# Longer TensorE filler and three moved steps around the gate columns of an mLSTM block (two-layer decoder, one core)

## The reference

```python
x = ln(x + causal_attention(x))
x = ln(x + cross_attention(x, ctx, mask))
x = ln(x + sign_mlp(x))                  # 256 -> 1024 -> 1024 -> 256, weights +1 and -1
x = ln(x + performer(x))                 # causal linear attention, 16 heads
x = ln(x + mlstm(x, ctx, ctx))
x = ln(x + quantised_conv_mlp(x))

def mlstm(q, k, v):
    gate_in = concatenate([q, k, v], -1)
    it = gate_in @ Wi_w.T + Wi_b;  ft = gate_in @ Wf_w.T + Wf_b
    csum = cumsum(log_sigmoid(ft), over tokens)
    D = where(causal, csum_i - csum_j + it_j, -inf)
    max_d = max(D, -1);  D = exp(D - max_d)
    C = (q_h @ k_h.T) * D / sqrt(32)
    H = C @ v_h / (max(abs(sum(C, -1)), exp(-max_d)) + 1e-6)
    return group_norm(H per head) * gn_w + gn_b
```

## Time and profile before

| | |
|---|---|
| median of 3 runs | 926.52 us |
| lowest and highest | 925.8 and 930.36 us |
| the profiled execution | 926.52 us, span 925.3 us |
| mean granted clock of TensorE | 0.949 of 2.4 GHz |
| PE, PEld busy | 767.2 us (83%), 512.0 us (55%) |
| DVE, ACT, POOL busy | 601.5 us (65%), 368.4 us (40%), 147.0 us (16%) |

### The profile page before, as it was taken

The page is one execution under the profiler, slowest core; times in us unless marked ns, Lnnn a source line. Parts: engine busy times, 40 slices in busy tenths (PEclk is TensorE's granted clock), DMA queues, the critical chain, the costliest instruction groups (busy, mean ns, idle before and its releaser), DMA issues.

```text
span 925.3 us, 14796 instructions
## 1 busy us (share of the span) xinstructions
PE 767.2 (83%) x5905; PEld 512.0 (55%) x5954; DVE 601.5 (65%) x1485; ACT 368.4 (40%) x654; POOL 147.0 (16%) x236
## 2 busy tenths in 40 slices
PE   8789977899999887899999877899999878675234
PEld 5554535666765654666765455666755456455112
DVE  1653733336876788647776788547767698457696
ACT  2563122125641265236532365246522364251072
POOL 4110010011412200011502200011412100113200
PEclk9998999999999999999899999999999999969568
DMA  9410000020010000030010000100100000000000
GB/s 357 155 46 1 0 24 1 2 69 23 1 46 1 1 24 1 2 113 1 1 46 1 1 24 2 53 17 1 47 1 1 0 2 1 23 1 1 0 1 23
DMA packets 13508, 25.86 MB, mean 28 GB/s; under 512 B 768, under 2 KB 7040, under 8 KB 13184
## 3 DMA queue, kind: packets, MB, share of 16 engines
q1 hardware_dynamic: 13440, 24.92, 7.7%
HBM read 22.82 MB, written 2.10 MB: 27 GB/s over the span
## 4 chain that ended last, share of the span: by engine, by line
PE 63%; DVE 22%; ACT 8%; issue 4%; another core or an unknown queue 1%; POOL 1%; DVEq 0%; ACTq 0%
PE bank L977 12%; PE bank L818 7%; PE bank L826 5%; PE bank L869 3%; PE bank L987 3%; PE bank L1072 3%; PE bank L965 3%; PE bank L1264 2%; PE bank L849 2%; DVE work L1642 2%; PE bank L1020 2%; DVE work L1857 1%; PE bank L804 1%; PE bank L1054 1%
## 5 line engine op out<-in xcount | busy, mean ns | idle before, releaser
L2214 POOL TENSOR_TENSOR rstd<-rstd,minus_half 128x2 f32<-128x2 f32 x56 | 44.2, 791 | 455.4 <-DVE rstd L1373 455.4
L977 PE MATMUL bank<-work,f0w 128*128 128x512 f16 x512 | 111.7, 379 | 0.0
L977 PEld LDWEIGHTS bank<-work,f0w 128*128 128x128 f16 x512 | 50.2, 98 | 59.7
L2052 ACT ACTIVATE work<-bank 128x512 f16<-128x512 f32 x64 | 37.8, 595 | 100.2 <-PE bank L977 80.9
L804 PE MATMUL bank<-bar_upper,identb 128*128 128x512 bf16 x117 | 37.6, 437 | 37.5 <-DVE x L1382 12.7
L1561 DVE SCALAR_TENSOR_TENSOR work<-bank,work 128x512 f16<-128x512 f32 x64 | 42.3, 687 | 29.6 <-ACT work L2052 29.6
L1445 DVE TENSOR_REDUCE small<-bank 128x1 f32<-128x512 f32 (+3 forms) x32 | 18.6, 582 | 63.9 <-PE bank L850 50.0
L869 PE MATMUL bank<-work 128*128 128x256 f32 x208 | 49.8, 383 | 1.8 <-ACT work L1990 1.8
L2090 ACT ACTIVATE work<-bank 128x512 f32<-128x512 f32 x32 | 18.9, 591 | 67.7 <-PE bank L1072 67.7
L2287 POOL TENSOR_TENSOR small<-small,minus_half 128x8 f32<-128x8 f32 x16 | 26.2, 1639 | 112.8 <-DVE small L1788 112.8
L804 PEld LDWEIGHTS bank<-bar_upper,identb 128*128 128x128 bf16 x138 | 13.3, 107 | 55.4 <-issue 12.8
(11 more groups left out here) (271 smaller groups left out, 1761.2 us busy)
## 6 DMA issues: line engine op xcount, KB each, us to landing
ctxT<-in_ctxT SPq DMA_DIRECT2D x8, 512.0 KB, 4.7
work<-in_mask SPq DMA_DIRECT2D x4, 1024.0 KB, 5.9
xT<-in_xT SPq DMA_DIRECT2D x4, 512.0 KB, 3.6
work<-in_w SPq DMA_DIRECT2D x1, 2048.0 KB, 18.7
ctx<-in_ctx SPq DMA_DIRECT2D x4, 512.0 KB, 3.8
out<-y SPq DMA_DIRECT2D x4, 512.0 KB, 3.1
perf_w<-in_perf_w SPq DMA_DIRECT2D x1, 1536.0 KB, 15.9
x<-in_x SPq DMA_DIRECT2D x2, 512.0 KB, 7.4
```

Of the source, the lines that this page charges most:

```text
L977: ins = nc.tensor.matmul(u.bank[:, :], f0w1[:, k, m * P:(m + 1) * P], h1[part][:, k, :], start=(k == 0 and part == 0), stop=(k == NF - 1 a ...
L2052: nc.scalar.activation(dst[0][:, m, :], u.bank[:, :], ACT.Relu).then_inc(high_made.sem, 1)
L2214: nc.gpsimd.tensor_tensor(s.rstd[:, two], s.rstd[:, two], minus_half[:, 0:2], ALU.pow).then_inc(s.rstd_made.sem, 1)
```

## The change

Four edits, all in the mLSTM block.

1. TensorE, ahead of the small products: the wait for the key gates is replaced by the one for the largest gates, which stood behind the filler.
2. The filler has three matmuls more: 6 in samples 0 to 2, 9 in sample 3.
3. VectorE: the three products dM move from behind `nmd` to behind part 3.
4. ScalarE: the step `part3` (the copy of part 2 into its place) moves ahead of the step `raw1` (the four copies of the second raw group).

```diff
             yield "mlstm.cols"
             u = bb["mlstm", b, "cols"]
-            pe.wait_ge(*key_gates.at(b))
+            pe.wait_ge(*gates_final.at(b))
             if b == B - 1:
-                keep_clock(fb["perf", b, "out", 1], 6, False)
+                keep_clock(fb["perf", b, "out", 1], 9, False)
                 pe.wait_ge(*u.free)
             else:
-                keep_clock(u, 3)
-            pe.wait_ge(*gates_final.at(b))
+                keep_clock(u, 6)
             pe.wait_ge(*diagonals.at(b))
...
             yield "mlstm.nmd"
             dve.wait_ge(*gates_final.at(b))
             vec.mark(nc.vector.tensor_tensor(nmd[0:LH, :], negM[0:LH, :], csum[0:LH, :], ALU.subtract))
-            for t in range(1, NT):
-                ins = nc.vector.tensor_scalar(dM[:, t - 1, :], ident[0:LH, 0:LH], negM[0:LH, t * P - 1:t * P], None, ALU.mult)
-            ins.then_inc(diagonals.sem, 1)
             yield "mlstm.part2"
...
             nc.vector.tensor_tensor(parts[64:64 + LH, :, :], rest[0:LH, :, :], part2_row, ALU.subtract).then_inc(part3.sem, 1)
+            for t in range(1, NT):
+                ins = nc.vector.tensor_scalar(dM[:, t - 1, :], ident[0:LH, 0:LH], negM[0:LH, t * P - 1:t * P], None, ALU.mult)
+            ins.then_inc(diagonals.sem, 1)
...
             nc.scalar.copy(parts[0:LH, :, :], gm[0:LH, :, :]).then_inc(part1.sem, 1)
-            yield "mlstm.raw1"
-            raw_scores(1)
             yield "mlstm.part3"
             act.wait_ge(*part2.at(b))
             nc.scalar.copy(parts[32:32 + LH, :, :], part2_row).then_inc(part2_placed.sem, 1)
+            yield "mlstm.raw1"
+            raw_scores(1)
             yield "mlstm.weigh"
```

## The result

| | before | after |
|---|---|---|
| median of 4 runs each, taken together | 926.16 us | 936.75 us |
| lowest and highest | 925.55 and 930.36 us | 933.99 and 942.2 us |
| the profiled execution | 926.52 us, span 925.3 us | 931.51 us, span 930.2 us |
| mean granted clock of TensorE | 0.949 | 0.951 |

The ratio of after to before is 1.0102, interval 1.0059 to 1.0146: the change makes the kernel slower by 1%, some 9 us. The forecast was 924.7 us in a range of 921.5 to 931.5. The traced execution of after is not among its four runs and lies at the low end (the same kernel built a second time ran from 931.31 to 942.09 us), so its trace shows the mechanism, but less than the full loss.

The account below looks back on a forecast made before the run. The prediction took TensorE to set the pace in samples 0 to 2, VectorE close behind, with time lost at 1.2 GHz. It summed 926.52 + 1.35 + 1.9 - 4.6 - 0.5 = 924.7 us, range 921.5 to 931.5.

Parts of the forecast that it names:

- What bounds the kernel: Around the change in samples 0 to 2, TensorE sets the pace, with VectorE close behind; 0.15 us of waiting in sample 2.
- gave back 0.5 us: Samples 0 to 2: of 5.1 us of clock gain, 0.5 returns as waiting on VectorE, leaving -4.6.
- The delays in samples 0 to 2: Ahead of the small products: the earlier copy adds 0.45 us per sample (+1.35), three more filler matmuls +1.9 over three samples.
- The clock in samples 0 to 2, -4.6: Around the small products: three of four parts of 6.8 us lost to 1.2 GHz are kept, less waiting on VectorE.
- those of being wrong: Listed signs: clock mean still 0.57 in all three stretches, sample 3 small products 5.2 us, or TensorE's wait before L1264 growing.
- dM in samples 0 to 2, nothing: VectorE's dM behind part three delays the front half's normalising by 0.48 us; costed at nothing, as TensorE asks later.
- Sample 3, -0.5: Small products start 1.95 us later, but nine filler matmuls restore 2.4 GHz, so they end at 827.5: -0.5 us.
- all three late inputs: Sample 3: filler, dM and the emptied raw bank all ready only at 824.6 to 824.75, holding the small products.
- hands a shift on whole: Sample 3: VectorE paces the heads without a gap from 830.2, 1.08 us each, and passes any shift on unchanged.
- The second: Slower rival: small products drop the clock regardless and sample 3 starts 1.95 us late at 1.2 GHz; 931.8 to 932.5, chance 0.17.
- The third: Wash rival: half of 6.8 us kept, VectorE and ScalarE give part back at the values, sample 3 even; 927.9, chance 0.26.
- the first: All-kept rival: clock kept everywhere, 926.5 + 3.25 - 6.8 - 0.9 = 922.0 us, chance 0.15.

Follow-up runs that it names:

- e13: All four edits in samples 0 to 2 only, against the kernel before; median 932.18 us, ratio 1.0055.
- e16: The kernel before with VectorE's head multiply cut to half of its columns; median 924.28 us, ratio to before 0.9956.
- e17: All four edits in samples 0 to 2 only, with VectorE's head multiply cut to half of its columns; median 923.84 us, ratio to before 0.9968.
- e7: dM moved behind part 3 in samples 0 to 2 only, against the kernel before; median 930.09 us, ratio 1.0029.
- e14: All four edits in sample 3 only, against the kernel before; median 931.2 us, ratio 1.0036.
- e5: The changed kernel unaltered, built and timed again against the kernel before; median 935.98 us, ratio 1.0088.
- e6: dM moved behind part 3 in sample 3 only, against the kernel before; median 932.08 us, ratio 1.0055.
- e12: Copy of part 2 moved ahead of the second raw group in sample 3 only, against the kernel before; median 931.5 us, ratio 1.0054.
- e3: dM moved behind part 3 in all samples, nothing else, against the kernel before; median 935.33 us, ratio 1.0087.
- e9: The kernel before, unaltered, timed and traced a second time; median 927.7 us, ratio 1.0002.
- e11: Moved gate wait and six filler matmuls in every sample, against the kernel before; median 932.09 us, ratio 1.0037 without its run of 942.38 us.
- e8: Copy of part 2 moved ahead of the second raw group in samples 0 to 2 only, against the kernel before; median 929.12 us, ratio 1.0017.
- e10: Moved gate wait, nine filler matmuls in sample 3 and three in the others, against the kernel before; median 926.48 us, ratio 1.0002.

## Why the prediction was wrong

**What bounds the kernel** was read half right. TensorE does set the pace up to the values, but the prediction took from the lack of a wait in the earlier trace rows that it also sets it when it gets faster. The 0.15 us of waiting in sample 2 came in a sample that had already lost 3.4 us of clock: it says that VectorE was just as late as a TensorE with that loss. Nothing was left to gain from keeping the clock over such a stretch. The sum gave back 0.5 us where all but 1.3 us had to be given back, even if every fall had been avoided: samples 0 and 2 of before took 14.79 and 14.84 us from small products to values, sample 1 took 16.17, and a kept clock makes each 14.86.

**The delays in samples 0 to 2** were right in size: 0.45 for the copy and 0.63 for the filler were forecast, 1.13 us in all were measured. They were right in place too: they move VectorE's multiplies with them, and so are paid even though a kept clock is not. Up to the values after lost 2.6 us over the three samples; in the means these samples lose 5.1 (e13), where 3.25 less 4.6 were forecast.

**The clock in samples 0 to 2, -4.6, is the term that failed most.** Its measured size up to the values is -0.8 us in after's trace (2.6 less 3.4). It failed twice. One fall of three was avoided in after's trace, not three quarters of them; over all traces six fillers kept the clock in 7 of 15 samples, and three in 6 of 30. And the price per us of clock was wrong: the 1.7 us of TensorE's time that a stretch of 3.4 us at half the clock takes were counted as 1.7 us of the kernel, less a little, while on the way to the values such a stretch costs between -0.2 and 0.3 us, and only one of 6.8 us costs 1.3. e16 and e17 show that the cause is VectorE's multiply. The prediction had named the sign of this among those of being wrong, a wait for VectorE before L1264 that grows by what the clock gives, and it is what sample 1 shows with its 1.69 us.

**dM in samples 0 to 2, nothing,** was right: e7 gives 1.0029 with zero on the edge, and its trace has every stretch of these samples within 0.01 us of that of e14, where dM stands as before.

**Sample 3, -0.5,** came out in after's trace: 0.53 us less from raw scores to values, the small products 2.0 us late and then at 2.4 GHz, and all three late inputs where they were forecast. But that was in part luck. The prediction had one trace of this stage, with 20.58 us, and four of eight traces of the same code take 17.7; and of the traces with all edits there, e14 has 22.96. Against the mean of the eight (19.1) after and e5 are 0.9 us late. The step from there to the end failed as well. That VectorE "hands a shift on whole" was taken to mean that the tail behind it stays as long. It did not: 88.4 us instead of 86.6 in after, 88.5 in e5 and 88.7 in e14, where the eight traces have 85.7 to 88.1, and the mean of the runs with all edits in sample 3 alone is 3.1 us up (e14). e6 and e12 give +5.3 and +5.0 for a late start alone.

**The rivals.** The second, 931.8 to 932.5, came nearest in time and in kind: with the delays paid and the clock not repaid. Its decision point, "as soon as less than 1 of the 6.8 us comes back", was met (0.8), but by VectorE's pace and not by a clock that nothing could keep; its other half, sample 3 low, did not come in after and e5, but did in e14. The third had the mechanism (VectorE gives it back at the values) and gave it 1.5 of 3.4 us. None of them had the part behind the values, which is why all ended short of 936. The 0.9 in the sum of the first has no working in the prediction, and no run shows it.

**What stays open.** In the means samples 0 to 2 lose 5.1 us and sample 3 loses 3.1. Of the 5.1, some 2.5 lie before the values in the traces (2.6 in after, 2.5 in e13). The rest is lost behind them, in falls of the clock beside the front half (162.6 us instead of 160.9 ahead of the gates of sample 2 in after, in e5 and in e13; 165.9 instead of 161.0 ahead of those of sample 1 in e5). These falls go with the pause of 1.69 us before the values. In samples 0 and 1 of all twenty traces, the 31 without that pause take 160.9 to 161.0 us from the values to the next gates, every one; of the nine with it, five take 162.5 to 165.9. The other four do not, and the trace of e7 has one of them in sample 0,

```profile
257.51 1.94 PE L1264 MATMUL bank<-work 128*128 128x66 f32 x16 [1.69 <-DVE work L1730]
```

in a kernel run of 920.5 us of span, one of the shortest seen. Behind sample 2 it is 143.2 us in the four traces with the pause (e3, e6, e9, e12) and 141.7 to 142.2 in the others, but for one of 143.8 (e11). e17 fits too: its two kept samples have no pause and take 160.95 and 160.97 us to the next gates. So the pause comes before the loss but does not always bring it, and why is not shown. The tail differs between 85.7 and 88.1 us among traces whose sample 3 is that of before (85.7 in e8, 88.1 in e9), so a part of it is the run's own luck.

## What to carry over

Before a faster clock (or any faster engine) is priced, take the engine that the next join waits for: if it was within 0.2 us of being last while the first engine ran slowly, a faster first engine gains nothing, and what is spent to get it is paid in full. Filler costs its length wherever its queue is the path, so leave it out first and time that, sample by sample; here three matmuls fewer in three samples gave 0.5%, and what six in the serial stage are worth stayed within the noise. In a serial stage, where nothing runs beside, put the small step that others wait for ahead of the large one; starting 2 us late cost 5 us in the mean here. And read more than one trace of the kernel before: its first trace hid that the same code keeps the clock in some samples, and that its stage in sample 3 takes 2.9 us less in half of the traces.

## What was not expected of the hardware

- One kernel ran from 921.6 to 933.3 us, a spread of 1.3%, with nothing changed; its two traces (spans of 925.3 and 929.4 us) differ in where the stretches at 1.2 GHz fall. Two traces of the changed kernel were 7.8 us apart. From the start to the gates of sample 0, where no kernel is edited, the twenty traces took from 215.7 to 223.3 us.
- The clock fell though TensorE had records without a gap, or all but: in all three like stretches of before, and for 10 us in e5 from 262.8 us on, there 0.8 us behind a wait of 1.69 us. In samples 0 and 2 of before the work just ahead of the fall is 2.8 us of matmuls of 8 rows and 8 to 72 columns; in sample 1 it fell 1 us into them.
- A 3.4 us stretch at 1.2 GHz cost nothing that the values show, and one twice as long 1.3 us: half of a loss is free when a neighbour is just behind.
- In sample 3 the clock came back within the filler in some traces and not in others, with either length: with nine wide matmuls in after (their 8 records span 2.32 us) but not in e10 (4.02 us), and with six in e8 (2.08 us) but not in before. The number of matmuls does not decide it alone.
